# Moving a key transpose and a quarter of a query projection to later places in TensorE's order of one attention stage

## The reference

```python
x = x + _L0_attn_ref(_L0_cond_ref(x, ...), ...)      # layer 0
x = x + _L0_ffn_ref(_L0_cond2_ref(x, ...), ...)
x = x + _L1_attn_ref(_L1_cond_ref(x, ...), w_qkv, w_o)   # the stage of the change
x = x + _L1_ffn_ref(_L1_cond2_ref(x, ...), ...)      # paged attention, then a quantised feed-forward part

def _L1_attn_ref(hidden_states, w_qkv, w_o):     # 32 query heads, 8 key heads, head size 128
    qkv = hidden_states @ w_qkv
    ...
    scores = jnp.einsum('bqhgd,bkhd->bhgqk', q, k) * scale
    attn = jax.nn.softmax(scores + bias[None], axis=-1)
    out = jnp.einsum('bhgqk,bkhd->bqhgd', attn, v).reshape(B, S, NH * D)
    return out @ w_o
```

## Time and profile before

| what | value |
|---|---|
| median of 3 runs | 2228.58 us (2221.11, 2228.58, 2229.07) |
| the profiled execution's own time | 2221.11 us, span in the trace 2219.3 us |
| PE busy | 2049.7 us, 92% of the span |
| DVE, ACT, POOL busy | 1571.6, 1306.4, 794.0 us |
| granted TensorE clock, mean | 0.964 of full speed |

### The profile page before, as it was taken

How to read it: one execution, slowest core, us unless ns; L and a number is a source line. 1 busy time by engine, 2 the same in 40 slices (tenths; PEclk the granted TensorE clock), 3 DMA queues, 4 the chain that set the end, 5 groups by cost and what they waited for, 6 DMA issues and landing times.

```text
span 2219.3 us, 35419 instructions
## 1 busy us (share of the span) xinstructions
PE 2049.7 (92%) x12261; PEld 1715.9 (77%) x12280; DVE 1571.6 (71%) x3479; ACT 1306.4 (59%) x3765; POOL 794.0 (36%) x779
## 2 busy tenths in 40 slices
PE   6999977999999999989999999999999999999744
PEld 5777656888888888778888888888888888888621
DVE  5576744555555555577888888878888888888787
ACT  3676643444444444456677767767777677777421
POOL 4100005000000000056666666665666666566231
PEclk9999998999999999999999999999999999999955
DMA  8101101100100110121111211111111111121100
GB/s 283 48 25 44 49 1 67 46 26 26 48 30 21 46 48 2 52 73 33 58 49 32 77 32 59 51 31 62 44 59 51 32 59 51 29 67 32 31 10 29
DMA packets 39362, 106.03 MB, mean 48 GB/s; under 512 B 10242, under 2 KB 15618, under 8 KB 34834
## 3 DMA queue, kind: packets, MB, share of 16 engines
q1 hardware_dynamic: 22802, 70.17, 8.9%
q0 software_dynamic: 16384, 33.59, 5.3%
HBM read 101.63 MB, written 2.10 MB: 47 GB/s over the span
## 4 chain that ended last, share of the span: by engine, by line
PE 84%; DVE 10%; ACT 3%; issue 1%; DMA 0%; POOL 0%; SPq 0%; DVEq 0%; ACTq 0%; POOLq 0%
PE PS L1433 9%; PE PS L1445 8%; PE PS L1342 8%; PE PS L1213 7%; PE PS L1273 7%; PE PS L1400 7%; PE PS L1418 6%; PE PS L1356 4%; PE PS L1226 4%; PE PS L1403 3%; PE PS L344 2%; PE PS L1241 2%; PE PS L1258 2%; PE PS L488 2%; PE PS L334 1%; PE PS L1248 1%
## 5 line engine op out<-in xcount | busy, mean ns | idle before, releaser
L2011 POOL DMA_INDIRECT kcache<-in_kcache,rows x256 | 252.6, 987 | 564.6 <-DVE x_res L1527 494.1
L1663 DVE CUSTOM_DVE_ANT_0 pr<-PS,ffn_weights,sm 128x640 f32<-128x640 f32 x256 | 225.4, 886 | 133.9 <-PE PS L1403 133.9
L2019 POOL DMA_INDIRECT vcache<-in_vcache,rows x256 | 259.5, 1014 | 136.6 <-PE PS L1241 61.0
L1931 ACT ACTIVATE pr<-pr,sm 128x640 f32<-128x640 f32 x256 | 213.1, 833 | 43.7 <-DVE sm L1663 43.7
L1679 DVE TENSOR_TENSOR prT_lo<-PS,prT_hi 128x512 fp32r<-128x512 f32 x320 | 209.6, 686 | 40.3 <-ACT prT_hi L1942 39.2
L1942 ACT ACTIVATE prT_hi<-PS 128x512 fp32r<-128x512 f32 x320 | 178.5, 596 | 67.2 <-PE PS L1418 59.2
L2025 POOL TENSOR_TENSOR vcached_lo<-vcache,vcached_hi 128x512 fp32r<-128x512 f32 x64 | 83.3, 1301 | 275.9 <-ACT vcached_hi L1914 275.9
L1418 PE MATMUL PS<-consts,pr 128*128 128x128 f32 x1280 | 173.3, 273 | 6.8 <-DVE prT_lo L1679 4.6
L1418 PEld LDWEIGHTS PS<-consts,pr 128*128 128x128 f32 x1280 | 150.1, 141 | 32.0 <-DVE prT_lo L1679 6.3
L1804 ACT ACTIVATE pr<-pr,sm 128x128 f32<-128x128 f32 x256 | 99.9, 392 | 118.2 <-DVE sm L1517 118.2
L1400 PE MATMUL PS<-kT_lo,qT_hi 128*128 128x320 f32 x512 | 154.1, 309 | 0.0
(11 more groups left out here) (310 smaller groups left out, 6271.3 us busy)
## 6 DMA issues: line engine op xcount, KB each, us to landing
arena<-in_wqkv SPq DMA_DIRECT2D x16, 1536.0 KB, 7.0
arena<-in_wo SPq DMA_DIRECT2D x16, 1024.0 KB, 5.6
arena<-in_wcT SPq DMA_DIRECT2D x8, 1024.0 KB, 5.7
kcache<-in_kcache,rows POOLq DMA_INDIRECT x256
vcache<-in_vcache,rows POOLq DMA_INDIRECT x256
arena<-in_xT SPq DMA_DIRECT2D x8, 256.0 KB, 6.2
x_res<-in_x SPq DMA_DIRECT2D x1, 2048.0 KB, 14.5
ffn_weights<-in_alibi SPq DMA_DIRECT2D x2, 1024.0 KB, 6.6
```

The costliest lines, as they stand in the source:

```text
L1663: dve.tensor_tensor_reduce(pr2[:, h, :].rearrange("p (a n) -> p a n", a=2), PS[:, SCORE_BANK[h]:SCORE_BANK[h] + 2, 0:HALF], keymask[:, b, ...
L1931: act.activation(pr2[:, h, :], pr2[:, h, :], ACT.Exp, bias=nm2[:, h:h + 1], scale=-1.0, accum_out=rs2[:, h:h + 1]).then_inc(a2_ex, 1)
L2011: pool.indirect_dma_start(out=kcache[:, c, :], out_offset=None, in_=T["kcache"], in_offset=bass.IndirectOffsetOnAxis(ap=rows[:, g, b, c:c ...
L2019: pool.indirect_dma_start(out=vcache[:, c, :], out_offset=None, in_=T["vcache"], in_offset=bass.IndirectOffsetOnAxis(ap=rows[:, g, b, c:c ...
```

## The change

In TensorE's `step1`, `turn_probs1(i)` comes straight behind `project_out1(i - 1)`. The query projection is cut in two halves in place of 1, 2 and 1 quarters: one half between `turn_probs1` and `weigh1`, the other behind `weigh1`. `turn_k1(i + 1)` moves from behind `turn_probs1` to behind `weigh1`. In ScalarE's `step1`, `kT_copy1(i + 1)` moves from behind `hi_of_probs1(i)` to behind `hi_of_o1(i)`. No instruction is added or taken away.

```diff
@@ TensorE, step1
+                turn_probs1(i)
                 n = i + 1 + GH
-                if 3 <= i and n < ITEMS:
-                    project_q_head(n, (0,))
-                elif i == ITEMS - 3:
-                    project_q(0, (0,))
-                turn_probs1(i)
-                if i + 1 < ITEMS:
-                    turn_k1(i + 1)
                 if i == 0:
                     ffn_out(B - 1, 5)
                 elif i < 3:
                     project_q_head(2 * i + 2)
                 elif n < ITEMS:
-                    project_q_head(n, (1, 2))
+                    project_q_head(n, (0, 1))
                 elif i == ITEMS - 3:
-                    project_q(0, (1, 2))
+                    project_q(0, (0, 1))
...
                 weigh1(i)
+                if i + 1 < ITEMS:
+                    turn_k1(i + 1)
                 if i == 0:
                     last_conv()
                 elif i < 3:
                     project_q_head(2 * i + 3)
                 elif n < ITEMS:
-                    project_q_head(n, (3,))
+                    project_q_head(n, (2, 3))
                 elif i == ITEMS - 3:
-                    project_q(0, (3,))
+                    project_q(0, (2, 3))
@@ ScalarE, step1
                 hi_of_probs1(i)
-                if i + 1 < ITEMS:
-                    kT_copy1(i + 1)
...
                 hi_of_o1(i)
+                if i + 1 < ITEMS:
+                    kT_copy1(i + 1)
```

## The result

The changed kernel takes 2263.19 us (median of 4 runs, 2258.59 to 2267.4), the kernel before 2225.72 us in the same comparison (4 runs, 2221.11 to 2229.07). The medians differ by 37.5 us; the recorded ratio is 1.0175, with a 95% interval of 1.0155 to 1.0196 (the medians alone give 1.0168). The forecast was 2260 us and slower, in a range of 2245 to 2274. The profiled execution took 2256.67 us, with a span of 2254.9; that of before had 2219.3, so 35.6 us are to be found between two traces. Lines of `kernel.py` moved by up to four: VectorE's L1522 of before is L1518 after, and ScalarE's L1799 is L1795.

The account below looks back on a forecast made before the run. TensorE's waits were taken to bound the kernel. 28.0 for 50 ordinary steps, 1.4 for seven weight items and 4.2 for four bare items made 33.6, say 34 us: 2255 or 2262.6 by starting time, predicted 2260, range 2245 to 2274.

Parts of the forecast that it names:

- The place of the limit: Stage of the change, about 330 to 960 us: time is lost where TensorE waits; VectorE and ScalarE loads do not matter.
- The cover ahead of the transposes: Quarter query head ahead of `turn_probs1` hides the softmax's end; without it a new stall of 0.40 us per step.
- The cover ahead of the weighing: Between `turn_probs1` and `weigh1`: without the key's transpose the stall is 0.30 where it was 0.18, 0.12 us more.
- The sum for a step: An ordinary step grows by 0.54 us, 0.40 + 0.12 of it stalls; taken as 0.56, 28.0 for 50 steps.
- The key's copy: `kT_copy1` behind `hi_of_o1`: key ready about 0.86 us after the weighing, hidden by 1.50 of TensorE work in ordinary steps.
- the bare items: Items 0, 59, 60 and 62, without query work behind the weighing: scores wait for the key's copy, 1.06 us each, 4.2 together.
- The seven items with new output weights: Items such as 8, where VectorE and ScalarE split the weights: only 0.20 us more each, 1.4 for seven.
- The end of the stage: Last items: 57, 58 and 61 counted as ordinary at 0.56 us, bare items 59, 60 and 62 at 1.06 each.
- The clock in the middle of the stage: Rival: two gaps per step also lower the clock; about 2274 us if once per key head, over 50 more otherwise; 6%.
- The cheap case: Rival: transposes lose only the 0.19 us wait, weighing's wait stays 0.18; step grows 0.2, kernel 2237 to 2244; 8%.
- the faster one: Rival: probabilities ready before TensorE's 5.11 us of work, so the new order fills the weighing's wait; 2219 us; 3%.

Follow-up runs that it names:

- one matmul in front: Against the changed kernel: one of the query head's 12 matmuls back ahead of the transposes (1, 6, 5); 2254.37 us, ratio 1.0127.
- The run with the quarters alone: Against the changed kernel: the key's transpose and copy go back, only the query quarters stay moved; 2246.4 us, ratio 1.0093.
- The run with the key's copy first: Against the kernel before: key's transpose behind the weighing, its copy just ahead of the output's copy, quarters 3, 6, 3; 2236.28 us, ratio 1.0044.
- 0.33 with 0.69 of cover: Against the kernel before: only the key's transpose and copy move, behind the weighing and the output's copy; 2261.43 us, ratio 1.0166.
- 0.10 with 0.94: Against the changed kernel: two of the 12 matmuls back ahead of the transposes (2, 6, 4); 2245.18 us, ratio 1.0093.
- The run with the bare items in the old order: Against the changed kernel: items 0, 59, 60 and 62 keep the key's transpose and copy in the old places; 2256.99 us, ratio 1.0157.
- the kernel cut 2, 7, 3: Against the kernel before: query head's 12 matmuls cut 2, 7, 3 instead of 3, 6, 3, key's work untouched; 2214.64 us, ratio 0.9959.

## Why the prediction was right

**The place of the limit** was read rightly: where TensorE waits, the kernel is longer, and the other engines' loads did not matter: VectorE and ScalarE are busy for 1571.3 and 1306.1 us, as before. The growth was forecast at 33.6 us and came out at 37.5 by the medians, 35.6 between the traces. That 2260 lies only 3 us from 2263 owes a little to the starting time: it stood for a kernel of 2226.4, between the 2221.1 and 2228.6 then known, and the median of four came to 2225.7.

**The cover ahead of the transposes.** The stall was priced at 0.40. Changed, the transposes end at 558.47, and the product was there 0.71 before that (0.70 at item 9); with one matmul in front 0.24 of the stall went, with two the transposes were back at 0.44. The run with the quarters alone gives 0.43 for the step (9.70 less 9.27), as was expected.

**The cover ahead of the weighing.** Priced at 0.12. The weighing went from 0.87 to 0.96, and with the 0.02 ahead of it in the chain the wait grew by 0.11. The run with the key's copy first isolates it: 9.38 less 9.27 is 0.11.

**The sum for a step.** 0.56 was used, and 0.56 is the difference of the medians (9.83 less 9.27); for items 3 to 57 that made 27.7 us (47 ordinary steps and seven of 0.20), and 28.5 came. The key's transpose among wide matmuls costs 0.11, the value that I had taken between nothing and more.

**The key's copy.** Forecast as hidden in ordinary steps. ScalarE's timeline of the changed kernel confirms it:

```profile
560.88 0.60 ACT L1811 ACTIVATE oT_hi<-PS 128x512 fp32r<-128x512 f32 x1 [1.77 <-PE PS L1258]
561.37 0.27 ACT L1795 ACTIVATE pr<-PS 128x128 f32<-128x128 f32 x1
```

The copy is done at 561.64, 0.80 after the weighing's end at 560.84; the scores begin 0.5 after that. The text said "if that cover is gone it costs the difference": two runs show this in ordinary steps (0.33 with 0.69 of cover, 0.10 with 0.94), and the bare items show it at 1.1 each.

**The seven items with new output weights.** 0.20 each was forecast. From item 8's softmax product to item 9's it is 10.16 us before and 10.17 changed; the step behind it goes from 9.02 to 9.83. For the pair that is 0.82, where 0.20 + 0.56 was forecast: right within 0.06, but with a split that was off. By the chain of waits, from item 8's transposes to item 9's it is 9.70 before (435.15 to 444.85) and 10.18 changed (439.14 to 449.32), 0.48 more; the forecast's 9.86 started from a record that begins 0.16 ahead of the end of the one before it. The scores begin 4.64 after the transposes, where 4.6 was forecast, and then take 1.14 in place of 0.89. From item 9's transposes to item 10's only 0.34 came on top (9.48 and 9.82), since item 9's had waited before the change too. These scores wait for the key's copy, as the working for item 8 had it; its list of what the profile would show forgot them ("elsewhere no wait there"). Item 56, the seventh, has no query part to split and grew by 0.22 (9.61 to 9.83).

**The end of the stage** is the term that was sized too small: three ordinary steps (1.7) and three bare items (3.2), 4.9 us, where 8.1 came. The run with the bare items in the old order splits it. The key's copy in the three bare items is the 4.06 that it gave back (10.05, 14.97 and 15.45 became 8.95, 13.25 and 14.21), where 3.2 was forecast; most of the excess is at item 60, 1.72, where the clock is low. The items with `turn_x` were counted as ordinary at 0.56. There the exponentials also wait for ScalarE's copy of `x`. In the changed kernel the chain of waits goes through it at 930.93, and the path from the scores to the product takes 5.87 (928.14 to 934.01) in place of 5.26, while the transposes of `x` give TensorE only 0.45 more to do meanwhile. The quarter had hidden that too. The steps behind items 57, 58 and 61 went from 9.61, 9.70 and 9.73 to 10.45, 10.44 and 10.43: 2.28. The remaining 1.8 had no place in the sum. Of it 1.04 lies in items 59 and 60, where the clock fell at another item, and 0.74 in item 62, whose excess was not taken apart. The weighing of item 60, before and changed, and the clock behind the latter:

```profile
927.23 0.50 PE L1258 MATMUL PS<-prT_hi,vown_hi 128*128 128x512 f32 x1 [3.04 <-DVE prT_lo L1536]
...
958.35 0.79 PE L1258 MATMUL PS<-prT_hi,vown_hi 128*128 128x512 f32 x1 [3.15 <-DVE prT_lo L1532]
...
962.00:965.00 3.00, 3.00 (x16) 3.00 (x16) 1.55 (x3) 0.00 (x0) 0.00 (x0) 0.50 0.02 5
```

0.50 of full speed, that is 1.2 GHz, after TensorE had stood 3.15 us for the low part of the probabilities at item 60. In the kernel before the clock fell after the 1.30 us gap at item 59, and not at item 60, where the gap was 3.04. The fall at item 59 cost 1.56 (10.51 before, 8.95 with the bare items in the old order, where it did not happen), the fall at item 60 cost 2.60 (13.25 with the bare items in the old order, 10.65 before). Why the fall is at one item and not the other was not settled. Item 0, the fourth bare item, cannot be read: items 0 to 3 take 47.81 us before, 47.66 changed and 44.82 with the bare items in the old order.

**The rivals.** The clock in the middle of the stage stayed at 1.00. The Trainium skill ("TensorE: Matmul & The Clock Gate", section "A second HAM failure mode: psum-queue depth-cycling") warns of frequent short idle spells; two waits a step, of 0.2 to 0.3 us, did not bring that on here: 1.00 from 400 to 900 us. The cheap case, 0.2 for a step, fell with the 0.66 of the transposes; the faster one fell with the path from scores to product, which did not shorten (562.34 to 567.60, 5.26 us; 5.25 in the prediction).

## What to carry to other kernels

In an order written out by hand, count for every wait how much independent work stands between the instruction that starts the path and the one that needs its end, and set it against the path's length: too little stalls, and more than enough is wasted cover that another wait could use. Moving a block by one wait takes its cover from one and gives it to the next, so two parts of a change can cost 19 and 34 us apart and 37 together. When the same work is cut in finer pieces (12 matmuls here in place of 4 quarters), the cover can be matched to each path, and that gave 0.4% with nothing added or taken away.

## What the runs showed of the hardware that was not expected

An instruction group that waits can pay more than its idle time. The four transposes end 0.71 us after the softmax product both when TensorE had stood idle for 0.19 (changed) and when it had not stood at all (one matmul in front: ready at 567.85, the product there at 567.80); they take 0.66 in both. 0.44 returned when TensorE came 0.28 after the product (two in front: 566.84 and 566.56), and there their first weight load had begun at 566.62, ahead of the end of the matmul in front. A wait of 0.09 us before the scores, as the chain shows it, cost 0.33 with the slower start behind it.

The table of waits is a measure of neither. In the changed kernel its row of matmuls for the transposes has 0.21 us an item (11.3 in 54), where the stall costs 0.40. The row of weight loads has 0.31 an item (16.7 in 54) in the kernel cut 2, 7, 3, where the wait costs nothing.
